# Patch embedding of a vision transformer: small inputs in whole rows, the weights' column sums as two rows in front of the images

## The chip, the cores and the metric

One core of a Trainium2 chip runs one program. The metric is the device time of one execution in microseconds (us). TensorE is written PE, VectorE DVE, ScalarE ACT, GpSimd POOL, SyncE SP. SP and ACT also issue the DMA transfers.

## The reference, cut to what matters

```python
# x: (16, 3, 96, 96) images, patches of 16x16 pixels, 6x6 per image
patches = x.reshape(B, C, h, P, w, P).transpose(0, 2, 4, 3, 5, 1).reshape(B, h * w, P * P * C)
y = _layernorm(patches, ln1_w, ln1_b)                 # over 768 numbers of a patch
y = jnp.einsum('bnp,pd->bnd', y, lin_w) + lin_b       # (768, 256)
y = _layernorm(y, ln2_w, ln2_b)
y = jnp.concatenate([cls, y], axis=1)                 # 37 tokens an image, 592 in all
y = y + pos_embedding[:, :n + 1]
...
h = _L0_tok_ref(...)
h = h + _L0_attn_ref(_layernorm(h), ...)              # 16 query heads, one key head
h = h + _L0_ffn_ref(_layernorm(h), ...)               # mixture of 8 experts, and a shared one
h = h + _L1_attn_ref(_layernorm(h), ...)              # three rounds over 16 heads, weights Wlq, Wlk, Wlv
h = h + _L1_ffn_ref(_layernorm(h), ...)               # quantised feed-forward
```

The change touches the first line of `h`, the patch stage, and the place at which products of the small matrices of `_L1_attn_ref` are made.

## The kernel before, in words

The program has one block for each engine, written out by hand in the order in which the engine runs it. There is no scheduler: engines meet at semaphores alone. PE writes into eight banks of PSUM, taken in a fixed order: `fills()` lists every fill of a bank with a key and the engine that empties it, fill n goes to bank n modulo 8, and `fill(key)` on PE first waits until fill n-8 is emptied. So the place of a key in the list sets who must have read what before PE may go on.

The first layer norm is folded into the embedding. The weights `lin_w` (six chunks `k` of 128 rows by 256) are scaled by `ln1_w` and a row of means is subtracted (`centred_weights`), and the patch's own rate 1/std is multiplied in behind the product (`rt`, `rtok`). The row of means and a constant row are column sums of `lin_w` weighted with `ln1_w` and `ln1_b`. The steps of the stage and their keys:

- `ln`: PE turns `ln1_w` and `ln1_b` into columns (`ln_cols`), ACT copies them.
- `ad`: a product of a 0/1 matrix (`token_of`) with `table` (position, class token and `ln2_b`, one row per token of an image) gives for each of five tiles of 128 tokens what is added to it (`addend`). DVE builds `table` in `make_table` once `pos_in` says that ACT's three small transfers have landed.
- `xp`: the patches of channel c are copied together by POOL (four of six columns of patches) and ACT (`windows`, two of six), turned by PE (four fills of three transposes each) and copied by ACT into `patT`.
- `cs`: the column sums. `mr`, `cr`: they are turned and spread over 128 partitions; ACT makes `mean_row` of the first, DVE `c_row` of the second.
- `y`: the embedding, tiles 0 and 1 chunk by chunk, then 2 and 3, then 4. `rt` stands between.
- `wl`, `wn`, `bl`: block-diagonal copies of Wlq, Wlk, Wlv, which DVE puts into `wlT`; `pw`: two rounds of products of them (their powers); `wc`: the key and query weights of the fourth stage multiplied with them; `xT`: the turned normalised tokens.

All loads of weights stand on SP's queue, ahead of the images or behind them, in the order of the code; nothing of the stage but the five small transfers is on ACT's queue.

Of the kernel before, what the change touches and what calls it, by code (L numbers as in the profile page):

```python
# [84 lines left out]
POOL_WINDOWS = 4  # L85

# [3 lines left out]
def fills():  # L90
# [21 lines left out]
    f.extend((("pw", n), "act") for n in range(2))  # L112
# [15 lines left out]
    f.extend((("wc", n), "act") for n in ("q", 1, 2, 3))  # L128
# [76 lines left out]
def build(nc, i, out):  # L205

    with ExitStack() as ctx:
# [3 lines left out]
        def sem(name):  # L211
            return ctx.enter_context(nc.semaphore(name))
# [13 lines left out]
        def cut(region, n):  # L226
            at[0] += n
            return region[:, at[0] - n:at[0]]
# [68 lines left out]
        col_sums = cut(cur, 4)  # L297
# [18 lines left out]
        r_lin, r_ln2w, r_ln2b = (sqr_all[:, n * D:(n + 1) * D] for n in range(3))  # L316
        rsd_all = sb("rsd", P, NR * CF)
        rsd = rsd_all[:, :].rearrange("p (n t) -> p n t", n=NR)
        token_all = rsd_all[0:T, 0:NP]
        token_of = rsd_all[0:T, 0:NT].rearrange("p (b t) -> p b t", t=T)  # L320
# [4 lines left out]
        table = probs_all[0:T, 0:DA]  # L325
        r_cls = probs_all[0:T, 2 * D:3 * D]
# [80 lines left out]
        weights_centred = sem("weights_centred")  # L407
        attn_cleared = sem("attn_cleared")
# [65 lines left out]
        def _(sp):  # L474
# [57 lines left out]
        def _(pool):  # L532
            links = [0]

            def link(ins):
                links[0] += 1
                ins.then_inc(pool_chain, 1)
                pool.wait_ge(pool_chain, links[0])
# [29 lines left out]
            link(pool.memset(token_all[:, NT:NP], 0.0))  # L568
            pool.tensor_copy(token_of, ident[0:T, 0:T].unsqueeze(1).to_broadcast([T, B, T])).then_inc(consts_ready, 1)  # L569
# [78 lines left out]
        def _(act):  # L648
# [44 lines left out]
            b = take(act, ("ln",))  # L693
            empty(act.copy(ln_cols.rearrange("p c v k -> p (c v k)"), b[:, 0:4 * NC]))
# [3 lines left out]
            windows(0)  # L698
            channel(0)
            b = take(act, ("cs",))  # L700
            empty(act.copy(col_sums, b[:, 0:4]))
            b = take(act, ("mr",))
            empty(act.mul(mean_row, b[:, 0:D], 1.0 / PV))
            for c in (1, 2):
                windows(c)
                channel(c)
# [39 lines left out]
            for n in range(2):  # L746
                powers(n)
# [57 lines left out]
            for n in ("q", 1, 2):  # L805
                composed_weights(n)
# [174 lines left out]
        def _(dve):  # L981
# [33 lines left out]
            def make_table():  # L1015

                dve.wait_ge(pos_in, 48)
                dve.tensor_reduce(table[:, D + 1:DA], ident[0:T, 1:T].rearrange("p (g w) -> p w g", g=NG), AX.X, ALU.add)  # L1018
                dve.tensor_scalar(first[:, 1:2], ident[0:T, 0:1], -1.0, 1.0, ALU.mult, ALU.add)
                link(dve.tensor_copy(first[:, 0:1], ident[0:T, 0:1]))  # L1020
                link(dve.scalar_tensor_tensor(out=table[:, 0:D], in0=r_cls, scalar=first[:, 0:1], in1=table[:, 0:D],
                                              op0=ALU.mult, op1=ALU.add))
                dve.tensor_copy(table[:, D:D + 1], first[:, 1:2])
                link(dve.scalar_tensor_tensor(out=table[:, 0:D], in0=r_ln2b[0:T, :], scalar=first[:, 1:2],
                                              in1=table[:, 0:D], op0=ALU.mult, op1=ALU.add))
                dve.tensor_copy(first[:, 0:1], ident[0:T, 0:1]).then_inc(table_ready, 1)  # L1026
# [58 lines left out]
            def rest_of_weights():  # L1085
                for k in range(4, PK):
                    centred_weights(k)
# [10 lines left out]
            variance_given(ins, rest_of_weights)  # L1098
# [579 lines left out]
        def _(pe):  # L1678
# [10 lines left out]

            def full(ins):  # L1690
                ins.then_inc(bank_filled, 1)
# [14 lines left out]

            b = fill(("ln",))
            keep_awake(b, 6)
# [5 lines left out]

            pe.wait_ge(table_ready, 1)
            for t in range(TT):
                b = fill(("ad", t))
                full(product(b[:, 0:DA], [(token_all[:, t * P:(t + 1) * P], table)]))
# [14 lines left out]
            channel(0)  # L1733
# [3 lines left out]
            for n in range(2):  # L1737
                ins = product(b[:, 2 * n:2 * n + 2], [(lin_w[:, k, n * P:(n + 1) * P], ln_cols[:, k // 2, :, k % 2]) for k in range(PK)])
            full(ins)
            emptied(pe, ("cs",))  # L1740
            for v, key in enumerate((("mr",), ("cr",))):
                b = fill(key)
                for n in range(2):
                    ins = pe.transpose(b[:, n * P:(n + 1) * P], col_sums[:, 2 * n + v:2 * n + v + 1].to_broadcast([P, P]), ident[:, :])
                full(ins)
            channel(1)
            channel(2)

# [20 lines left out]
            bs_ = [fill(("y", t)) for t in range(2)]  # L1769
            for k in range(PK):  # L1770
                pe.wait_ge(weights_centred, k + 1)
                for g in range(2):
                    emptied(pe, ("xp", k, g))
                for t in range(2):
                    ins = pe.matmul(bs_[t][:, 0:D], patT[:, k, t * P:(t + 1) * P], lin_w[:, k, :], start=(k == 0), stop=(k == PK - 1))  # L1775
                    if k == PK - 1:
                        full(ins)

# [8 lines left out]
            pe.wait_ge(image_of_ready, 1)  # L1787
# [25 lines left out]
            emptied(pe, ("bl",))  # L1813
            for n in range(2):
                if n:
                    emptied(pe, ("pw", 0))
# [158 lines left out]

            composed_weights("q", "q1", q_)
            for n in range(2):
                emptied(pe, ("pw", n))
            for a in (1, 2, 3):
                composed_weights(a, "k1", KEY_POWER[a - 1])  # L1980
# [258 lines left out]
```

## Time and profile before

| what | us |
|---|---|
| median of 3 runs | 324.23 (324.05 to 325.01) |
| the profiled execution, its time | 322.2 |
| the same, its span in the trace | 320.5 |
| PE busy in the span | 264.7 |
| DVE busy | 201.6 |
| ACT busy | 100.4 |
| POOL busy | 45.0 |

The span runs from the first to the last instruction of the program. The time has 1.7 us more around it. All times in the rows below are counted from the span's start. The granted clock of TensorE in the rows is a share of 2.4 GHz: 1.00 is the upper level, 0.50 is 1.2 GHz.

### The profile page before, as it was taken

How to read it: one execution, taken by the hardware profiler on the slowest of the kernel's cores; microseconds unless marked ns; L12 is line 12 of the kernel's file. 1: busy time of each engine (PE TensorE's matmuls, PEld its weight loads, DVE VectorE, ACT ScalarE, POOL GpSimd, SP SyncE). 2: the span in 40 equal slices, each digit the busy share in tenths (PEclk: the TensorE clock that was granted, in tenths of full speed). 3: DMA queues.
4: the chain of work that ended last, by engine and by line, in shares of the span. 5: the costliest groups of instructions: out<-in, count | busy, mean ns of one | idle time of the engine just before them, and what ended most of it. 6: DMA issues, size and time to landing. Idle time of an engine off the chain costs nothing.

```text
span 320.5 us, 5617 instructions
## 1 busy us (share of the span) xinstructions
PE 264.7 (83%) x2221; PEld 218.8 (68%) x2221; DVE 201.6 (63%) x485; ACT 100.4 (31%) x238; POOL 45.0 (14%) x88
## 2 busy tenths in 40 slices
PE   4039699678987989999999998998868899937496
PEld 3028688578977757777787798876646677717484
DVE  1051608953683536889788962786788846997931
ACT  1004610333224154211111253476330533917000
POOL 7140000020053000000000000679400000000000
PEclk9999979879557999999999986999999999987789
DMA  7919500500000043000000000000000000000011
GB/s 205 221 22 314 169 2 1 164 3 2 4 0 2 4 149 146 2 0 0 0 2 1 0 2 1 2 3 0 4 0 3 0 0 2 0 0 0 1 35 43
DMA packets 14524, 12.10 MB, mean 38 GB/s; under 512 B 2975, under 2 KB 13954, under 8 KB 14498
## 3 DMA queue, kind: packets, MB, share of 16 engines
q1 hardware_dynamic: 14376, 11.62, 12.3%
q8 instruction: 18, 0.29, 0.4%
q10 hardware_dynamic: 122, 0.12, 0.1%
q14 instruction: 8, 0.07, 0.1%
HBM read 11.13 MB, written 0.61 MB: 37 GB/s over the span
## 4 chain that ended last, share of the span: by engine, by line
PE 66%; DVE 18%; ACT 6%; DMA 5%; issue 3%; ACTq 1%; DVEq 0%
PE bank L1702 47%; DMA sqr<-in_L_tok_ln_b 5%; PE bank L2206 5%; PE bank L1865 3%; PE bank L1898 2%; DVE part L1546 2%; PE bank L1775 2%; PE bank L1929 2%; DVE big L1610 1%; DVE keys_n L1591 1%; PE bank L1840 1%; PE bank L1973 1%; DVE big L1644 1%; ACT xT L740 1%; PE bank L1729 1%
## 5 line engine op out<-in xcount | busy, mean ns | idle before, releaser
L1702 PE MATMUL bank<-xT,big 128*128 128x296 f32 (+1 forms) x192 | 45.7, 391 | 0.0
L1702 PEld LDWEIGHTS bank<-xT,big 128*128 128x128 f32 x192 | 34.3, 190 | 9.5 <-issue 0.2
L1702 PE MATMUL bank<-xT,fT 128*128 128x296 f32 (+12 forms) x96 | 24.6, 416 | 0.6 <-DVE xT L1567 0.6
L1702 PE MATMUL bank<-big,cur 128*128 128x256 f32 (+1 forms) x100 | 23.3, 381 | 0.7 <-DVE cur L1321 0.7
L822 ACT ACTIVATE cen<-bank 128x296 f32<-128x296 f32 x20 | 8.3, 418 | 46.4 <-PE bank L1702 40.7
L1697 PE MATMUL bank<-ident,ones 128*128 128x128 f32 x100 | 17.1, 340 | 6.2 <-POOL rsd L569 4.4
L1702 PEld LDWEIGHTS bank<-xT,fT 128*128 128x128 f32 x96 | 17.2, 191 | 7.1 <-issue 2.1
L1702 PEld LDWEIGHTS bank<-big,cur 128*128 128x128 f32 (+1 forms) x100 | 18.0, 182 | 4.9 <-DVE cur L1321 1.5
L1697 PEld LDWEIGHTS bank<-ident,ones 128*128 128x128 f32 x100 | 16.4, 253 | 6.6 <-POOL rsd L569 4.4
L1334 DVE SCALAR_TENSOR_TENSOR h<-bank,route,h 128x256 f32<-128x256 f32 (+1 forms) x40 | 17.0, 478 | 2.8 <-PE bank L1702 2.8
L624 POOL TENSOR_SCALAR big<-keys_n,k_w 128x256 f32<-128x256 f32 x24 | 17.5, 750 | 6.4 <-DVE keys_n L1425 6.4
L1546 DVE TENSOR_REDUCE part<-big 128x1 f32<-128x296 f32 (+2 forms) x18 | 13.1, 731 | 6.3 <-ACT big L958 6.3
L1702 PE MATMUL bank<-probs,rsd 37*128 37x263 f32 x10 | 4.7, 658 | 13.4 <-DVE first L1026 13.4
L2206 PE MATMUL bank<-fT,big 128*128 128x256 f32 (+1 forms) x60 | 15.2, 419 | 0.6 <-DVE big L1543 0.6
L2206 PEld LDWEIGHTS bank<-fT,big 128*128 128x128 f32 (+1 forms) x60 | 12.2, 206 | 3.4 <-DVE big L1543 0.8
L1702 PEld LDWEIGHTS bank<-probs,rsd 37*128 37x128 f32 x10 | 3.2, 327 | 14.4 <-DVE first L1026 13.5
L616 POOL COPY cur<-xT 128x256 f32<-128x256 f32 x2 | 0.8, 404 | 80.9 <-ACT xT L742 80.9
L1321 DVE TENSOR_TENSOR cur<-cen,bank 128x296 f32<-128x296 f32 x20 | 9.1, 461 | 4.8 <-PE bank L1702 4.4
L1702 PE MATMUL bank<-wT_o,att 128*128 128x256 f32 (+1 forms) x40 | 9.3, 383 | 1.5 <-DVE att L1502 0.9
L606 POOL TENSOR_TENSOR big<-big,row_sum 128x370 f32<-128x370 f32 x8 | 6.2, 813 | 24.8 <-DVE row_sum L1217 24.8
L1702 PEld LDWEIGHTS bank<-wT_o,att 128*128 128x128 f32 (+1 forms) x40 | 7.0, 182 | 3.1 <-DVE att L1502 1.3
L1018 DVE TENSOR_REDUCE probs<-ident 37x6 f32<-37x36 f32 x1 | 0.2, 208 | 14.2 <-DMA sqr<-in_L_tok_ln_b 14.2
(312 smaller groups left out, 540.2 us busy)
## 6 DMA issues: line engine op xcount, KB each, us to landing
big<-in_x SPq DMA_DIRECT2D x3, 576.0 KB, 11.8
big<-in_L_ffn_w_gate SPq DMA_DIRECT2D x2, 512.0 KB, 6.5
big<-in_L_ffn_w_up SPq DMA_DIRECT2D x2, 512.0 KB, 6.7
big<-in_L_ffn_w_down SPq DMA_DIRECT2D x1, 1024.0 KB, 5.5
small<-in_L_tok_lin_w SPq DMA_DIRECT2D x3, 256.0 KB, 5.5
small<-in_L_ffn_w_gate SPq DMA_DIRECT2D x1, 768.0 KB, 4.6
small<-in_L_ffn_w_up SPq DMA_DIRECT2D x1, 768.0 KB, 6.8
small<-in_L_ffn_w_down SPq DMA_DIRECT2D x1, 768.0 KB, 8.1
```

Of the source, the lines that this page charges most:

```text
L624: ins = pool.tensor_scalar(fkeys[a - 1][:, u, :, n, :], keys, k_w[:, a - 1, n:n + 1], 1.0, ALU.mult, ALU.mult)
L822: empty(act.activation(silu[:, c, :], b[:, 0:HP], ACT.Silu))
L1321: empty(dve.tensor_tensor(hid[:, e % 3, c * HP:(c + 1) * HP], silu[:, c, :], b[:, 0:HP], ALU.mult))
L1334: ins = dve.scalar_tensor_tensor(out=v, in0=src, scalar=route[0:n, t, e:e + 1], in1=v, op0=ALU.mult, op1=ALU.add)
L1546: return dve.tensor_reduce(part[:, n:n + 1], v, AX.X, ALU.max, apply_absolute_value=True)
L1697: pe.matmul(b[:, 0:P], ones[:, :], ident[:, :], start=True, stop=True)
L1702: ins = pe.matmul(out_, a_, b_, start=(n == 0), stop=(n == len(pairs) - 1))
L1775: ins = pe.matmul(bs_[t][:, 0:D], patT[:, k, t * P:(t + 1) * P], lin_w[:, k, :], start=(k == 0), stop=(k == PK - 1))
L1865: ins = pe.matmul(b[32 * j:32 * j + m, at_:at_ + 4 * T].rearrange("p (u c) -> p u c", u=2), w(k), xq[:, k, :, 2 * j * T:2 * (j + 1) * T], ...
L1898: ins = pe.matmul(bs_[j][:, (2 * t + s) * T:(2 * t + s + 1) * T], qT[rows, row:row + P], kT[rows, u, s * T:(s + 1) * T], start=True, stop= ...
L1929: ins = pe.matmul(b[32 * q:32 * q + 32, m * 2 * T:(m + 1) * 2 * T].rearrange("p (i t) -> p i t", i=2), vals[0:G3, 3 * u + g, s, h_, :], by ...
L2206: ins = pe.matmul(b[0:rows, 0:D], gate[:, o * NT + t * P:o * NT + t * P + rows], fT[2][:, o, :], start=(o == 0), stop=(o == FC - 1))
```

## The change

Four things are changed.

1. ACT's small transfers: position rows 0 to 31 and 32 to 36 as two transfers, the class token and `ln2_b` as one row each (rows 37 and 38 of `table`, which gets `TR` = 39 rows), and these ahead of `ln1_w` and `ln1_b`. `token_of` gets two more rows (from `row_of`, two short POOL instructions), so that the product `ad` adds class token and `ln2_b`; `make_table` keeps two instructions and waits for no transfer. PE waits for `pos_in` itself.
2. The column sums are two rows of 256 (`ln_cols` is the stationary operand, `lin_w` moves) in place of four columns of 128, and are spread with a product in place of two transposes.
3. `lin_w` is loaded ahead of the images, and `ad`, `ln`, `cs`, `mr`, `cr` stand ahead of all of `xp`. DVE centres chunks 0 to 3 (with the statistics of channel 1 between), POOL chunks 4 and 5. The embedding of tiles 0 and 1 begins with chunks 0 and 1 ahead of channel 2.
4. The two fills `pw` move from behind `wkvT` to between the fills `wc`.

```diff
-    f = [(("ln",), "act")]
-    f.extend((("ad", t), "act") for t in range(TT))
-    channel(0)
+    f = [(("ad", t), "act") for t in range(TT)]
+    f.append((("ln",), "act"))
     f.append((("cs",), "act"))
     f.append((("mr",), "act"))
     f.append((("cr",), "dve"))
+    channel(0)
     channel(1)
     channel(2)
...
-    f.extend((("pw", n), "act") for n in range(2))
...
-    f.extend((("wc", n), "act") for n in ("q", 1, 2, 3))
+    f.extend((key, "act") for key in (("pw", 0), ("wc", "q"), ("pw", 1), ("wc", 1), ("wc", 2), ("wc", 3)))
...
+            for n in range(NC):
+                sp.dma_start(lin_w[:, 2 * n:2 * n + 2, :], lw[n]).then_inc(patch_w_in, 16)
             for c in range(NC):
                 sp.dma_start(imv[0:96, c, :], im[c]).then_inc(images_in[c], 16)
-                if c == 0:
-                    for n in range(NC):
-                        sp.dma_start(lin_w[:, 2 * n:2 * n + 2, :], lw[n]).then_inc(patch_w_in, 16)
...
+            emptied(pool, ("ln",))
+            emptied(pool, ("mr",))
             pool.wait_ge(windows_pool, NC * POOL_WINDOWS)
+            for k in range(DVE_CHUNKS, PK):
+                v = lin_w[:, k, :]
+                link(pool.tensor_scalar(v, v, ln_cols[:, k // 2, 0, k % 2:k % 2 + 1], 1.0, ALU.mult, ALU.mult))
+                pool.tensor_tensor(v, v, mean_row, ALU.subtract).then_inc(weights_centred_pool, 1)
...
+            for lo, hi in ((0, 32), (32, T)):
+                act.dma_start(table[lo:hi, 0:D], i["L0_tok_pos_embedding"][0, lo:hi, :]).then_inc(pos_in, 16)
+            act.dma_start(table[T:T + 1, 0:D], i["L0_tok_cls_token"][0, 0:1, :]).then_inc(pos_in, 16)
+            act.dma_start(table[T + 1:TR, 0:D], i["L0_tok_ln2_b"].unsqueeze(0)).then_inc(pos_in, 16)
             for n, name in enumerate(("L0_tok_ln1_w", "L0_tok_ln1_b")):
                 act.dma_start(ln_rows[2 * n:2 * n + 2, :], i[name].rearrange("(k m) -> k m", k=2)).then_inc(ln_in, 16)
-            act.dma_start(table[:, 0:D], i["L0_tok_pos_embedding"][0, :, :]).then_inc(pos_in, 16)
-            act.dma_start(r_cls, i["L0_tok_cls_token"][0, 0, :].partition_broadcast(T)).then_inc(pos_in, 16)
-            act.dma_start(r_ln2b[0:T, :], i["L0_tok_ln2_b"].partition_broadcast(T)).then_inc(pos_in, 16)
...
-            channel_statistics(1)
             emptied(dve, ("mr",))
             emptied(dve, ("ln",))
-            for k in range(4):
+            for k in range(DVE_CHUNKS):
+                if k == 2:
+                    channel_statistics(1)
                 centred_weights(k)
             link(channel_statistics(2))
...
-            for n in range(2):
-                ins = product(b[:, 2 * n:2 * n + 2], [(lin_w[:, k, n * P:(n + 1) * P], ln_cols[:, k // 2, :, k % 2]) for k in range(PK)])
-            full(ins)
+            full(product(b[0:2, 0:D], [(ln_cols[:, k // 2, :, k % 2], lin_w[:, k, :]) for k in range(PK)]))
             emptied(pe, ("cs",))
             for v, key in enumerate((("mr",), ("cr",))):
                 b = fill(key)
-                for n in range(2):
-                    ins = pe.transpose(b[:, n * P:(n + 1) * P], col_sums[:, 2 * n + v:2 * n + v + 1].to_broadcast([P, P]), ident[:, :])
-                full(ins)
+                full(product(b[:, 0:D], [(ident[0:2, v:v + 1].to_broadcast([2, P]), col_sums)]))
+            channel(0)
             channel(1)
+            first_banks = [opened(("y", t)) for t in range(2)]
...
+            embedding_of_first(range(2))
             channel(2)
+            for t in range(2):
+                fill(("y", t))
+            embedding_of_first(range(2, PK))
```

PE before, from the column sums (`lin_w` is in tensor `small`, `patT` in `big`, the patches of channels 0 to 2 in `fT0` to `fT2`) to the first products of the embedding:

```order
L1702 MATMUL bank2<-cur,small 128x2 [waits patch_w_in,act_emptied]
L1702 MATMUL bank2<-cur,small 128x2 x11
L1744 MATMUL bank3<-ident,cur 128x128 [waits act_emptied]
...
L1729 MATMUL bank0<-ident,fT1 128x96 [waits act_emptied]
...
L1729 MATMUL bank3<-ident,fT2 128x96 [waits act_emptied,windows_act,windows_pool]
L1729 MATMUL bank3<-ident,fT2 128x96 x2
L1729 MATMUL bank4<-ident,fT2 128x96 [waits dve_emptied]
L1729 MATMUL bank4<-ident,fT2 128x96 x2
L1775 MATMUL bank5<-small,big 128x256 [waits act_emptied,weights_centred]
```

And PE in the change, from `ad` to the same place:

```order
L1707 MATMUL bank0<-probs,rsd 128x263 [waits pos_in,table_ready]
...
L1707 MATMUL bank6<-small,cur 2x256 [waits patch_w_in,act_emptied]
L1707 MATMUL bank6<-small,cur 2x256 x5
L1707 MATMUL bank7<-cur,ident 128x256 [waits act_emptied]
L1707 MATMUL bank0<-cur,ident 128x256 [waits act_emptied]
...
L1735 MATMUL bank7<-ident,fT1 128x96 [waits act_emptied,windows_act,windows_pool]
L1735 MATMUL bank7<-ident,fT1 128x96 x2
L1735 MATMUL bank0<-ident,fT1 128x96 [waits dve_emptied]
L1735 MATMUL bank0<-ident,fT1 128x96 x2
L1761 MATMUL bank5<-small,big 128x256 [waits weights_centred,act_emptied,image_of_ready]
L1761 MATMUL bank6<-small,big 128x256
```

The fill that waits for DVE to empty `cr` was the last of channel 2, `fT2` into bank 4; now it is the last of channel 1, `fT1` into bank 0, with two chunks of the embedding and all of channel 2 behind it.

DVE in the change, from the statistics of channel 0 to `c_row`, which empties `cr`:

```order
L1069 BN_STATS st<-big 96x6 [waits images_in0]
L1069 BN_STATS st<-big 96x6 x5
L1073 SCALAR_TENSOR_TENSOR small<-small,cur 128x256 [waits act_emptied]
L1073 SCALAR_TENSOR_TENSOR small<-small,cur 128x256
L1069 BN_STATS st<-big 96x6 [waits images_in1]
L1069 BN_STATS st<-big 96x6 x5
L1073 SCALAR_TENSOR_TENSOR small<-small,cur 128x256 x2
L1069 BN_STATS st<-big 96x6 [waits images_in2]
L1069 BN_STATS st<-big 96x6 x5
L1085 BN_AGGR mv<-st 96x2 [waits dve_chain]
L1085 BN_AGGR mv<-st 96x2 x5
L1090 TENSOR_TENSOR cur<-bank0,sqr 128x256 [waits bank_filled,norm_rows_in]
```

Before, the statistics of channels 0 and 1 stood ahead of the wait for `mr`, four chunks followed it, then channel 2, the six aggregates, two more chunks and `c_row`.

## Rows read from the trace of the kernel before

**Rows 1.** Chain of work that ended last: start us, us, what.

```profile
2.47 17.11 DMA sqr<-in_L_tok_ln_b
...
21.25 4.75 PE bank L1702 x10
...
28.21 4.98 PE bank L1702 x24
...
34.58 1.67 DVE small L1072 x4
36.25 1.98 DVE st L1068 x6
...
38.40 0.55 DVE mv L1083 x5
...
39.68 0.35 DVE cur L1090
...
47.43 8.90 PE bank L1702 x46
```

**Rows 2.** DMA queues from 8 to 12 us: packets, MB, share of 16 engines.

```profile
q10 hardware_dynamic: 29, 0.03, 3.2%
```

**Rows 3.** The page's DMA issues: KB each, median us to landing.

```profile
big<-in_x SPq DMA_DIRECT2D x3, 576.0 KB, 11.8
small<-in_L_tok_lin_w SPq DMA_DIRECT2D x3, 256.0 KB, 5.5
```

**Rows 4.** Timeline to 66 us: start, us, engine, line, operation, [idle before <-releaser].

```profile
3.52 0.13 POOL L568 MEMSET rsd<- 37x48 f32 x1
4.44 2.93 PE L1697 MATMUL bank<-ident,ones 128*128 128x128 f32 x12 [4.44 <-POOL rsd L569]
7.30 0.50 PE L1712 MATMUL bank<-ident,cur 4*128 4x4 f32 x3
22.56 0.47 SPq L503 DMA_DIRECT2D gate_w<-in_L_ffn_gate_w  x1
34.34 2.97 PE L1729 MATMUL bank<-ident,fT 96*128 96x96 f32 x18
40.07 0.47 PE L1729 MATMUL bank<-ident,fT 96*128 96x96 f32 x3 [1.75 <-DVE cur L1090]
40.37 7.06 PE L1775 MATMUL bank<-small,big 128*128 128x256 f32 x24
```

**Rows 5.** PE's line of the first embedding, two stretches: PE busy, records, granted clock.

```profile
40.50:43.70 3.20, 3.20 (x8) 0.50 0.02 5
44.00:47.20 3.20, 3.20 (x16) 1.00 0.00 0
```

**Rows 6.** Timeline, 62 to 70 us.

```profile
62.59 1.69 DVE L1043 TENSOR_SCALAR xn<-h,mv,rstd 128x256 f32<-128x256 f32 x5
62.73 1.65 PE L1702 MATMUL bank<-wlT 128*128 128x128 f32 x6 [2.82 <-DVE bl L1117]
67.25 1.52 PE L1840 MATMUL bank<-ident,xn 128*128 128x128 f32 x10
68.20 1.54 ACT L740 COPY xT<-bank 128x256 f32<-128x256 f32 x6 [1.08 <-PE bank L1840]
```

**Rows 7.** The chain again, the query projections.

```profile
69.84 8.88 PE bank L1865 x271
```

**Rows 8.** PE's line L1929 alone (32 columns a piece), two stretches, as in rows 5.

```profile
98.50:101.80 3.30, 3.30 (x121) 0.50 0.02 5
105.80:107.90 2.10, 2.10 (x128) 1.00 0.03 8
```

**Rows 9.** Timeline, the fills `wc` of the second place.

```profile
111.16 3.73 PE L1702 MATMUL bank<-wlT,small 128*128 128x128 f32 x32
114.53 0.29 ACT L672 ACTIVATE var<-mv,eps_c 128x5 f32<-128x5 f32 x1
```

**Rows 10.** Timeline, POOL and DVE together in the fourth stage.

```profile
202.69 2.88 POOL L624 TENSOR_SCALAR big<-keys_n,k_w 128x256 f32<-128x256 f32 x3
202.78 1.99 DVE L1393 TENSOR_TENSOR big<-keys_n,k_w 128x1536 f32<-128x1536 f32 x1
```

More of the change, by code:

```diff
@@ L85 @@
 POOL_WINDOWS = 4
+DVE_CHUNKS = 4
+TR = T + 2
 def fills():
@@ L315, in build @@
         sqr = sqr_all[:, :].rearrange("p (n t) -> p n t", n=NR)
-        r_lin, r_ln2w, r_ln2b = (sqr_all[:, n * D:(n + 1) * D] for n in range(3))
+        r_lin, r_ln2w = (sqr_all[:, n * D:(n + 1) * D] for n in range(2))
         rsd_all = sb("rsd", P, NR * CF)
         rsd = rsd_all[:, :].rearrange("p (n t) -> p n t", n=NR)
-        token_all = rsd_all[0:T, 0:NP]
-        token_of = rsd_all[0:T, 0:NT].rearrange("p (b t) -> p b t", t=T)
+        token_all = rsd_all[0:TR, 0:NP]
+        token_of = rsd_all[0:TR, 0:NT].rearrange("p (b t) -> p b t", t=T)
         cmpa, cmpb = (rsd_all[:, n * TT * NE * NE:(n + 1) * TT * NE * NE].rearrange(
@@ L324, in build @@
         probsT = [x[0:G3, 0:3 * R].rearrange("p (g r) -> p g r", g=3) for x in (cur, probs_all)]
-        table = probs_all[0:T, 0:DA]
-        r_cls = probs_all[0:T, 2 * D:3 * D]
+        table = probs_all[0:TR, 0:DA]
+        row_of = probs_all[0:TR, 2 * D:2 * D + T]
         fprobs, fheads = (probs_all[:, n * 2 * CF:(n + 1) * 2 * CF].rearrange(
@@ L407, in build @@
         weights_centred = sem("weights_centred")
+        weights_centred_pool = sem("weights_centred_pool")
         attn_cleared = sem("attn_cleared")
@@ L567, in _ @@
             pool.memset(h[64:P, TT - 1, :], 0.0)
-            link(pool.memset(token_all[:, NT:NP], 0.0))
-            pool.tensor_copy(token_of, ident[0:T, 0:T].unsqueeze(1).to_broadcast([T, B, T])).then_inc(consts_ready, 1)
+            pool.memset(token_all[:, NT:NP], 0.0)
+            pool.tensor_tensor(row_of[:, 0:1], ident[0:TR, 0:1], ident[0:TR, T:T + 1], ALU.add)
+            link(pool.tensor_tensor(row_of[:, 1:T], ident[0:TR, 1:T], ident[0:TR, T + 1:TR].to_broadcast([TR, T - 1]), ALU.add))
+            pool.tensor_copy(token_of, row_of.unsqueeze(1).to_broadcast([TR, B, T])).then_inc(consts_ready, 1)
             pool.memset(patT_bt[:, :, :, 0], 0.0)
@@ L691, in channel @@
                         empty(act.copy(patch_columns(k, g), patches_turned(b)))
-            b = take(act, ("ln",))
-            empty(act.copy(ln_cols.rearrange("p c v k -> p (c v k)"), b[:, 0:4 * NC]))
             for t in range(TT):
@@ L697, in _ @@
                 empty(act.copy(addend[:, t, :], b[:, 0:DA]))
-            windows(0)
-            channel(0)
+            b = take(act, ("ln",))
+            empty(act.copy(ln_cols.rearrange("p c v k -> p (c v k)"), b[:, 0:4 * NC]))
             b = take(act, ("cs",))
-            empty(act.copy(col_sums, b[:, 0:4]))
+            empty(act.copy(col_sums, b[0:2, 0:D]))
             b = take(act, ("mr",))
             empty(act.mul(mean_row, b[:, 0:D], 1.0 / PV))
-            for c in (1, 2):
+            for c in range(NC):
                 windows(c)
@@ L803, in weight_turned @@
                     empty(act.copy(fT[2][:, 2 * j:2 * j + 2, :], b[:, :].rearrange("p (c o) -> p c o", c=2)))
-            for n in ("q", 1, 2):
-                composed_weights(n)
+            powers(0)
+            composed_weights("q")
+            powers(1)
+            composed_weights(1)
+            composed_weights(2)
             inverse_root(P, slice(0, TT))
@@ L1015, in make_table @@
             def make_table():
[L1017 to L1026, printed above, removed]
+                dve.tensor_reduce(table[:, D + 1:DA], ident[0:TR, 1:T].rearrange("p (g w) -> p w g", g=NG), AX.X, ALU.add)
+                dve.tensor_copy(table[:, D:D + 1], ident[0:TR, T + 1:TR]).then_inc(table_ready, 1)
             def statistics(ts):
@@ L1083, in _, with constant_row @@
                 ins = dve.bn_aggr(mv[0:96, w, :], st[0:96, 3 * w:3 * w + 3, :].rearrange("p a b -> p (a b)"))
-            def rest_of_weights():
-                for k in range(4, PK):
-                    centred_weights(k)
+            def constant_row():
                 dve.wait_ge(norm_rows_in, 32)
@@ L1688, in fill, with opened @@
                 return banks[n % 8]
+            def opened(key):
+                emptied(pe, FILLS[FILL[key] - 8][0])
+                return bank_of(key)
             def full(ins):
@@ L1705, in _ @@
             pe.wait_ge(consts_ready, N_CONSTS)
+            for t in range(TT):
+                b = fill(("ad", t))
+                if t == 0:
+                    keep_awake(b, 4)
+                    pe.wait_ge(table_ready, 1)
+                    pe.wait_ge(pos_in, 64)
+                full(product(b[:, 0:DA], [(token_all[:, t * P:(t + 1) * P], table)]))
             b = fill(("ln",))
-            keep_awake(b, 6)
             pe.wait_ge(ln_in, 32)
@@ L1713, in _ @@
             full(ins)
[L1715 to L1718, printed above, removed]
             def channel(c):
@@ L1731, in channel @@
                         full(ins)
-            channel(0)
             b = fill(("cs",))
@@ L1742, in _, with embedding_of_first @@
                 b = fill(key)
-                for n in range(2):
-                    ins = pe.transpose(b[:, n * P:(n + 1) * P], col_sums[:, 2 * n + v:2 * n + v + 1].to_broadcast([P, P]), ident[:, :])
-                full(ins)
+                full(product(b[:, 0:D], [(ident[0:2, v:v + 1].to_broadcast([2, P]), col_sums)]))
+            channel(0)
             channel(1)
+            first_banks = [opened(("y", t)) for t in range(2)]
+            def embedding_of_first(ks):
+                for k in ks:
+                    if k < DVE_CHUNKS:
+                        pe.wait_ge(weights_centred, k + 1)
+                    else:
+                        pe.wait_ge(weights_centred_pool, k + 1 - DVE_CHUNKS)
+                    for g in range(2):
+                        emptied(pe, ("xp", k, g))
+                    for t in range(2):
+                        ins = pe.matmul(first_banks[t][:, 0:D], patT[:, k, t * P:(t + 1) * P], lin_w[:, k, :],
+                                        start=(k == 0), stop=(k == PK - 1))
+                        if k == PK - 1:
+                            full(ins)
+            pe.wait_ge(image_of_ready, 1)
+            embedding_of_first(range(2))
             channel(2)
+            for t in range(2):
+                fill(("y", t))
+            embedding_of_first(range(2, PK))
             def small_matrices():
@@ L1767, in small_matrices @@
                 full(product(b[:, 0:2 * NH], [(bq8.rearrange("p n d -> p (n d)"), ident[0:2 * NH, 0:2 * NH])]))
[L1769 to L1777, printed above, removed]
             def embedding(ts):
@@ L1785, in embedding @@
                 full(ins)
-            pe.wait_ge(image_of_ready, 1)
             b = fill(("rt",))
@@ L1812, in _, with powers @@
             q_, k_, v_, nk, nv = range(5)
[L1813 to L1816, printed above, removed]
+            def powers(n):
                 b = fill(("pw", n))
@@ L1974, in weight_turned @@
                 full(ins)
+            emptied(pe, ("bl",))
+            powers(0)
             composed_weights("q", "q1", q_)
[L1977 to L1980, printed above, removed]
+            emptied(pe, ("pw", 0))
+            powers(1)
+            composed_weights(1, "k1", KEY_POWER[0])
+            composed_weights(2, "k1", KEY_POWER[1])
+            emptied(pe, ("pw", 1))
+            composed_weights(3, "k1", KEY_POWER[2])
             turn(1, 2)
```

5 lines of the change are left out of this document (2 added, 3 removed).

## Prediction

> **What bounds the kernel now.** I read the chain of waits first, since the change is at the program's start. Its first piece says it all: ACT's last small transfer (`ln2_b`, 37 rows) is issued at 2.47 us and landed 17.11 us later, at 19.6 [rows 1]. PE waits for the table made of it; the product `ad` starts at 21.25 and from there the chain runs on PE with short pieces of ACT and DVE. Next I asked why 111 rows of 1 KB take so long. ACT's queue (q10) moves 29 packets in the four microseconds from 8 to 12 [rows 2], one in 0.14 us: a row at a time, one behind the other. The weights `lin_w` (three transfers of 256 KB) need 5.5 us each in the same crowd, the images 11.8 us in the median [rows 3].
>
> The Trainium skill says why (DMA: Bandwidth & Descriptors, section "Why a DMA increments its semaphore by 16 and not by 1"): a transfer runs on the largest number of engines up to 16 that divides its slowest dimension, so 37 rows run on one and 32 on 16. The trace agrees for 37, by the drip just shown; for 32 nothing here shows it.
>
> Third, the timeline of PE up to 66 us [rows 4]. To about 37 us PE is slow: 18 transposes of 96 columns take 2.97 us, 0.16 each, while three at 40.07 take 0.47 in all, tails included. The clock rows say 1.00 there, but the durations say 1.2 GHz. At 40.07 PE resumes after 1.75 us in which a bank waited for DVE to read `cr`; behind it 24 records of the embedding run at 0.40 us apiece under a granted clock of 0.50 and at 0.20 under 1.00 [rows 5]. The embedding ends near 56.3 us (47.43 and 8.90, rows 1).
>
> **The change, step by step, on the clock of the profiled execution.**
>
> *Start of `ad`.* POOL has two more short instructions and a link ahead of `token_of`: a short one beside it takes 0.13 us [rows 4], so I take 0.35 us, and PE starts at 4.8 in place of 4.44. Four warming products are 8 records of the 12 that took 2.93 us: 1.95 us, so 6.75. `ad` can start then, if the table has landed. Now 32 rows, then 5, then 1 and 1 are ahead of all else on ACT. At one packet in 0.14 us even all 39 rows in one file last 5.5 us from an issue at 0.8: 6.3, plus a start of some 1 us that I read off the first landings (PE had `ln` at 7.30 at the latest). I take 6.75, bound by PE; the high bound is 9. `ad` takes 4.75 us as before [rows 1] and ends at 11.5. Before, this was 26.0.
>
> *To `mean_row`.* `ln` 0.50 [rows 4], ACT's copy 0.2: 12.2. `cs`: 12 records with 256 moving columns, as many as the embedding's. At 0.43 (low clock) 5.1, plus 0.2: 17.5. At the upper clock it would be 2.6. I take the low one, since what PE does ahead of it is what it did before at low speed. It replaces 4.98 us [rows 1], so the two-row form by itself is worth nothing. ACT's copy 0.4, one spread (2 records, tail) 1.05, ACT 0.4: `mean_row` stands at 19.45, in place of 34.58. **Minus 15.1 us** so far. `lin_w`, now first on SP, has landed some 5.5 us after its issue, 6 us early; the images, issued by 5 us and landing by about 16 as before, are early too.
>
> *The new stall.* This is the step that the short description does not tell. `xp` of channel 1 now ends in the bank of `cr`, which DVE empties last. From `mean_row` DVE has four chunks (1.67), statistics of channel 1 and of channel 2 (1.98 each, the second with a link of 0.15), aggregates 0.55 and `c_row` 0.35, with gaps 6.8 us [rows 1]. Before, it was 5.5, to 40.07. PE meanwhile has only the spread of `cr` and 21 transposes of 0.16, so it idles about 3 us. And POOL works on chunks 4 and 5 at the same time. Where POOL and DVE both read two things from SBUF, at 202.7, POOL's three take 2.88 us, 0.96 each, and DVE's 1.99 [rows 10]; so one of the two was held up. I add 0.5 us; the bounds are 0 and 1.9 (two of POOL's instructions). Resumption at 26.75 in place of 40.07: **minus 13.3**.
>
> The skill has a rule against this (SBUF — State Buffer, the rules on the shared port pair): a DVE instruction with two SBUF inputs and a GpSimd one that reads SBUF exclude one another for the whole instruction. By it the centring, not the statistics, could be held; the rows at 202.7 agree that something is, and my bounds already have room for it.
>
> *From there to the end of the first embedding.* Before, 3 transposes and 24 records took 40.07 to 47.27: 7.2 us, with the first 3.4 at low clock. Now 15 transposes and the same 24 records: at the upper clock 15 times 0.083 and 24 times 0.216, 6.45 us (0.083 is 0.16 halved with the clock, 0.216 is 5.2 over 24). PE comes from an idle stretch, as before, so the clock is low at first. The earlier case cost 1.7 us for it; I take 2.2, and 0.2 for latencies: 8.85. Ends at 35.6 in place of 47.27: **minus 11.7**. ACT has the last channel copied in that time: four copies and a `windows` are 2.7 us and PE gives it 6. `rt`, tiles 2 to 4 and everything on DVE behind them follow as before (8.90 us of PE, rows 1): the last of the attention's weights was issued at 22.56 [rows 4], by the 5.5 us above it had landed near 28, and is wanted after 44.
>
> *`pw` moved.* Its first fill held PE from 62.73 and the second ended near 66.6; then warming, and transposes at 67.25, though the first `xn` was there at about 63.0 [rows 6]. Now the transposes pace with `xn` (1.69 us for five): PE begins at 63.05, at low clock 10 records of 0.21 end at 65.3, ACT's copies (1.54 for all) at 65.9, and the projections can start at 66.1, not 69.84: minus 3.75. But what warmed the clock was `pw`. The projections, 8.88 us [rows 7], now start at low clock. Pieces of 32 columns run at 3.30 over 121 and 2.10 over 128, 27.3 and 16.4 ns, at the two levels [rows 8], so a low stretch loses 40% of its length. After the resumption at 40.07 the clock was low for 3.5 us or a little more; here I choose 4.7 us as the middle of 2.5 and 7, somewhat less and twice as much, for PE comes from sparse work. That costs 1.0 to 2.8; I take 1.9. At the new place the two fills, 12 records, stand ahead of the third `wc`, whose copy ACT must make ahead of the root that DVE waits for. There 32 records take 3.73, 0.117 each [rows 9]: plus 1.4. Together **minus 0.45**.
>
> **Sum:** minus 11.7 minus 0.45, 12.1 us. The profiled execution would be 322.2 minus 12.1, 310.1. It was 2.0 us under the median 324.23, so the median follows at **312.1**.
>
> **Rivals.**
>
> *Clock and port kinder.* Low clock nowhere longer than before, no hold by POOL, and `cs` partly at the upper level (PE then has 128 full rows moving, unlike before). Minus 2.2, 0.5, 1.9 and 1.0 at most; half to all of it gives 306.5 to 309.3. For it speaks that pieces at low clock were always followed by a rise when PE ran full (rows 5 and 8).
>
> *Low clock longer.* The projections all at low clock, or the embedding up to `rt`: 8.88 times 0.66 is 5.9, less the 1.9 counted, plus 4.0; the embedding the same, 12.6 less 8.85, plus 3.8. One gives 316. Against it: rows 8 rise with just such pieces.
>
> *Small transfers still late.* They now run beside 768 KB of `lin_w`. Each microsecond of landing behind 6.75 is one of the end. Landed at 10: 315.4. Landed at 19, as now, gives 324.4: the change would then not do what it says. Against it: 39 rows in place of 111.
>
> *Slower than before.* One mechanism: PE never leaves the low clock from the resumption to the end of the projections. The first embedding costs 3.8 more, `rt` and 36 records 8.9 more, the projections 4.0: 16.7, so 328.8. It decides once the low clock has cost 12.1 us more than counted, some 24 us of PE's work at half speed in a row. The rise by 44.0 in the same products [rows 5] speaks against it.
>
> **How the numbers follow.** The forecast has 0.55, with its own range of 309.5 to 314.5; kinder 0.17, longer low clock 0.17, late transfers 0.08 (of it 0.02 for no change), slower 0.03. The range 308.0 to 316.5 leaves out the best part of the kinder case and the worst of the late and slow ones, together under 0.2. Within 0.3% is within 1 us, about what a measurement of this kernel can tell. Faster 0.95, same 0.02, slower 0.03.
>
> **What would show it.** In the profile after: `ad` begins at 6.5 to 7.5 with no wait for a transfer; `cs` of 12 records lasts about 5 us; `mean_row` at 19 to 20; PE's wait for DVE's `c_row` of about 3 us, ending at 26 to 28, in the middle of channel 1; `rt` near 36; the projections start near 54, and their length is over 10 us. Wrong it would be by a wait of PE for `pos_in` behind 9 us, by a bank that I have not seen, or by a clock that stays at 0.50 in the embedding.

## The result, and the profile after

The changed kernel takes 309.58 us in the median of 4 runs (305.52 to 309.95), the kernel before 324.14 beside it (4 runs, 323.09 to 325.01): ratio 0.9524, 95% interval 0.9439 to 0.9608. Forecast were 312.1 and a range of 308.0 to 316.5. The profiled execution took 309.35 with a span of 307.6, 12.9 us under the span of 320.5 before; the sum had said 12.1. Run again (c0) it gave 308.40 against 322.69, ratio 0.9551 (0.9510 to 0.9593). Medians are of all executions, but ratios leave out those over 1.5% above the fastest of their kernel: two of e3's six (306.75 and 308.77), one of e7's six (304.88, the profiled one) and one of e5's four (508.8, the profiled one).

The chain of waits of the changed kernel, start, us and what, from the landing that opens it to the first projections; it answers to [rows 1]:

```profile
2.14 4.88 DMA probs<-in_L_tok_ln_b
...
7.16 4.72 PE bank L1707 x10
...
12.57 5.29 PE bank L1707 x12
...
19.45 1.10 DVE small L1073 x2
20.55 1.96 DVE st L1069 x6
22.51 0.78 DVE small L1073 x2
23.30 1.98 DVE st L1069 x6
...
26.34 0.74 PE bank L1735 x3
27.08 3.47 PE bank L1761 x8
30.55 1.58 PE bank L1735 x12
32.12 3.48 PE bank L1761 x16
35.61 8.90 PE bank L1707 x46
...
54.04 9.50 PE bank L1876 x272
...
93.38 6.86 PE bank L1707 x48
```

Read it against the old chain. The first piece was 17.11 us long and is 4.88. `ad` starts at 7.16 in place of 21.25. Then comes a stretch of DVE from 19.45 to 26.34, 6.9 us; in the old chain the same wait for `c_row` was 5.5 us long (34.58 to 40.07). PE has 21 transposes to do in it and is idle for the rest. The embedding of tiles 0 and 1 ends near 35.6, in place of 47.4 (`rt`, whose first product overlaps its end, starts at 35.44, in place of 47.27). The projections start at 54.04, not 69.84.

PE's timeline in the same kernel shows the wait itself, answering to [rows 4]:

```profile
19.36 1.84 PE L1735 MATMUL bank<-ident,fT 96*128 96x96 f32 x18
22.68 0.71 PE L1735 MATMUL bank<-ident,fT 96*128 96x96 f32 x3 [1.48 <-issue]
26.34 0.74 PE L1735 MATMUL bank<-ident,fT 96*128 96x96 f32 x3 [2.95 <-DVE cur L1090]
```

The last three transposes of channel 1 stand behind 2.95 us of idle time, ended by DVE's `c_row` (L1090). The 1.48 us ahead of 22.68 end with ACT's part of the channel's patches (its copy runs from 21.94 to 22.59); the profile names no releaser for them. The busy times by stretch give the clock (PE, PEld, DVE, ACT and POOL busy with their records, then the granted clock):

```profile
18.00:21.30 3.30, 2.90 (x22) 2.23 (x22) 1.85 (x5) 2.52 (x6) 1.62 (x3) 1.00 0.08 2
21.50:26.20 4.70, 0.71 (x3) 0.45 (x3) 4.67 (x19) 2.71 (x6) 2.88 (x5) 0.50 0.98 320
26.40:31.50 5.10, 5.10 (x19) 4.28 (x20) 0.00 (x0) 1.54 (x3) 0.00 (x0) 0.50 0.95 276
31.70:35.40 3.70, 3.70 (x21) 3.31 (x20) 0.00 (x0) 1.91 (x6) 0.00 (x0) 1.00 0.76 248
```

The clock was at the upper level behind the 12 wide records of `cs`: the 18 transposes at 19.36 take 0.10 us each, and at the low level they took 0.16. PE was then busy for 0.71 us of 4.70, the clock fell, and 5.1 us of full work ran at the low level before it rose.

### The profile page after: what moved, and what is told of

The parts are those of the page before. It is cut to its first block, busy times and chain, and to the rows that moved or that the text cites. A ratio compares the mean times of both kernels' runs of the same rounds, so it can differ in the third digit from the quotient of the medians.

```text
span 307.6 us, 5589 instructions
## 1 busy us (share of the span) xinstructions
PE 262.7 (85%) x2205; PEld 211.9 (69%) x2205; DVE 199.6 (65%) x478; ACT 100.4 (33%) x238; POOL 48.1 (16%) x94
## 4 chain that ended last, share of the span: by engine, by line
PE 68%; DVE 19%; ACT 6%; issue 3%; DMA 2%; ACTq 1%; DVEq 0%
PE bank L1707 49%; PE bank L2221 5%; PE bank L1876 3%; PE bank L1909 3%; DVE part L1546 2%; PE bank L1761 2%; PE bank L1940 2%; DMA probs<-in_L_tok_ln_b 2%; DVE big L1610 1%; DVE st L1069 1%; DVE keys_n L1591 1%; PE bank L1984 1%; DVE big L1644 1%; ACT big L980 1%; DVE xn L1044 1%
## 5 line engine op out<-in xcount | busy, mean ns | idle before, releaser
L1702 PE MATMUL bank<-ident,ones 128*128 128x128 f32 x96 | 15.7, 329 | 6.7 <-POOL rsd L572 4.8
L1702 PEld LDWEIGHTS bank<-ident,ones 128*128 128x128 f32 x96 | 14.7, 240 | 7.1 <-POOL rsd L572 4.8
L1851 PE MATMUL bank<-ident,xn 128*128 128x128 f32 x40 | 7.1, 305 | 4.1 <-DVE xn L1044 3.9
L1044 DVE TENSOR_SCALAR xn<-h,mv,rstd 128x256 f32<-128x256 f32 x20 | 7.0, 406 | 4.0 <-ACT rstd L683 4.0
L1909 PE MATMUL bank<-kT,qT 16*128 16x37 f32 x160 | 8.0, 374 | 1.1 <-ACT qT L763 1.1
```

Source lines behind the costliest of these rows:

```text
L1044: dve.tensor_scalar(xn[:, t, :], h[:, t, :], mv[:, t, 0:1], rstd[:, t:t + 1], ALU.subtract, ALU.mult).then_inc(xn_ready, 1)
L1702: pe.matmul(b[:, 0:P], ones[:, :], ident[:, :], start=True, stop=True)
L1851: ins = pe.transpose(b[:, at_:at_ + P], xn[:, t, k * P:(k + 1) * P], ident[:, :])
L1909: ins = pe.matmul(bs_[j][:, (2 * t + s) * T:(2 * t + s + 1) * T], qT[rows, row:row + P], kT[rows, u, s * T:(s + 1) * T], start=True, stop= ...
```

## The experiments

Each kernel was run beside the kernel before on its chip: c0 and e1 to e3 on one, e4 to e7 on another, e8 and e9 on a third. Kernels are compared by their ratio to it. Where a diff is cut, `...` marks it.

**The changed kernel again (c0), as yardstick.**

> The changed kernel once more, as the yardstick for its neighbours on the same chip. Both theories: 309.6, within the spread of the first runs (305.5 to 310.0).

308.40 (305.93 to 309.99), as expected.

**The transfers alone (e1).** The kernel before with part 1 and nothing else (of its diff, the transfers):

```diff
...
-            act.dma_start(table[:, 0:D], i["L0_tok_pos_embedding"][0, :, :]).then_inc(pos_in, 16)
-            act.dma_start(r_cls, i["L0_tok_cls_token"][0, 0, :].partition_broadcast(T)).then_inc(pos_in, 16)
-            act.dma_start(r_ln2b[0:T, :], i["L0_tok_ln2_b"].partition_broadcast(T)).then_inc(pos_in, 16)
+            for lo, hi in ((0, 32), (32, T)):
+                act.dma_start(table[lo:hi, 0:D], i["L0_tok_pos_embedding"][0, lo:hi, :]).then_inc(pos_in, 16)
+            act.dma_start(table[T:T + 1, 0:D], i["L0_tok_cls_token"][0, 0:1, :]).then_inc(pos_in, 16)
+            act.dma_start(table[T + 1:TR, 0:D], i["L0_tok_ln2_b"].unsqueeze(0)).then_inc(pos_in, 16)
...
```

> The kernel before with part 1 alone (small transfers in 32, 5, 1 and 1 rows, a table of 39 rows). Theory 'the transfer is all': PE warms with 12 records from 4.8 to 7.7, ln 0.5, ad starts at about 8.25 in place of 21.25, everything behind moves by 13.0 us: 324.1 - 13.0 = 311.1, and parts 2 and 3 together are worth nothing, since the resumption after the wait for c_row then comes at about 27.1. Rival 'the reordering carries part of it': with the images not ahead of the column sums the stage must be shorter; then this kernel is slower than the changed one by clearly more than the 1.7 us of the moved powers, 313 or more. A second rival: the later images become the bound once the table is early; then PE waits for POOL's patches behind ad.

308.51, ratio 0.9572 (0.9544 to 0.9601): the whole gain, within what can be told from the changed kernel's 0.9551. Both rivals fall. PE's timeline:

```profile
8.07 4.75 PE L1698 MATMUL bank<-probs,rsd 39*128 39x263 f32 x10
26.90 0.54 PE L1726 MATMUL bank<-ident,fT 96*128 96x96 f32 x3 [1.76 <-DVE cur L1086]
34.10 1.18 PE L1698 MATMUL bank<-rstd,cen 96*128 96x6 f32 x10
```

`ad` starts 0.9 us later than in the changed kernel and PE resumes 0.6 later, yet `rt` comes at 34.10, against 35.44 there. The old order leaves 3 transposes and 24 records behind the wait, the new one 15 and 24, with more of it at the low clock. So with this wait in place parts 2 and 3, the reordering of the stage, gained nothing, and in these profiles lost 1.3 us by this point.

What e1 doesn't separate: part 1 moves 39 rows in place of 111, replaces the two broadcasts by one row each, and takes DVE's work on the table (19.60 to 21.21, 1.6 us of the chain before) out of the way. `ad` starts 13.2 us earlier by all three; the broadcasts alone were not tried.

**`pw` back at its old place (e2).**

```diff
+    f.extend((("pw", n), "act") for n in range(2))
...
-    f.extend((key, "act") for key in (("pw", 0), ("wc", "q"), ("pw", 1), ("wc", 1), ("wc", 2), ("wc", 3)))
+    f.extend((("wc", n), "act") for n in ("q", 1, 2, 3))
...
```

> The changed kernel with the two fills pw back at their old place. The prediction's term (minus 0.45 for the move): 0.5 us slower than the changed kernel, about 310.1. The trace of the changed kernel (projections start 3.6 us earlier in relation to the end of the embedding, lose 0.6 to the clock, and the second place costs 1.34) says 1.7 us slower: 311.3. Rival: the clock decides and the move is worth nothing or less, 309.6 or under.

309.69, ratio 0.9621 (0.9586 to 0.9656), against 0.9551 for c0: 2.3 us worse by the ratios, 1.3 by the medians, and the intervals just touch. The chain of e2:

```profile
35.37 8.90 PE bank L1707 x46
...
58.22 9.06 PE bank L1881 x272
...
68.54 2.44 PE bank L1914 x80
...
95.77 5.52 PE bank L1707 x36
...
105.05 2.33 PE bank L1707 x8
```

and of c0:

```profile
35.40 8.90 PE bank L1707 x46
...
53.79 9.59 PE bank L1876 x272
...
64.50 3.46 PE bank L1909 x80
...
94.89 6.86 PE bank L1707 x48
...
105.51 2.33 PE bank L1707 x8
```

The move brings the projections forward by 4.4 us. Of this 0.5 is lost in the projections, 1.0 in the first scores and 1.4 in the 24 products behind them (4.18 us against 2.80), which run at a lower clock, and 1.34 at the new place; at the gate's products (105) this profile of the changed kernel is 0.46 us behind. So in one pair of profiles the move is worth nothing, in the medians one to two microseconds. Its sign is not settled; the forecast of minus 0.45 lies between.

e2 is also the kernel before with parts 1, 2 and 3, so beside e1 it weighs parts 2 and 3 alone. Its first embedding ends at 35.37 against 34.26, its projections start at 58.22 against 57.10, and its median is 309.69 against 308.51: 1.1 to 1.2 us slower each time.

**`c_row` ahead of the statistics of channel 1 (e3).**

```diff
                 if k == 2:
+                    dve.wait_ge(norm_rows_in, 32)
+                    b = take(dve, ("cr",))
+                    empty(dve.tensor_tensor(c_row, b[:, 0:D], r_lin, ALU.add))
                     channel_statistics(1)
...
-            def constant_row():
-                dve.wait_ge(norm_rows_in, 32)
-                b = take(dve, ("cr",))
-                empty(dve.tensor_tensor(c_row, b[:, 0:D], r_lin, ALU.add))
...
-            variance_given(ins, constant_row)
+            variance_given(ins)
```

> The changed kernel with DVE's c_row ahead of the statistics of channel 1, so that the bank of cr is empty at about 20.9 us. Theory 'a new stall': PE's idle 2.95 us in the middle of channel 1 goes, and the end of the first embedding comes 2 to 3 us earlier: 307. Rival 'it only moves': ACT's copies or the clock take what the stall gives up, 309 to 309.6.

304.02, ratio 0.9392 (0.9360 to 0.9425), better than c0 by 5.1 us by the ratios and by 4.4 us by the medians of all six executions of each; expected were 2 to 3. The stall was real. PE's timeline of e3:

```profile
21.98 1.19 PE L1733 MATMUL bank<-ident,fT 96*128 96x96 f32 x6 [1.18 <-issue]
23.11 3.75 PE L1759 MATMUL bank<-small,big 128*128 128x256 f32 x8
31.24 1.18 PE L1705 MATMUL bank<-rstd,cen 96*128 96x6 f32 x10
```

The wait for DVE is gone and `rt` starts at 31.24, 4.0 us before c0's 35.24. That is more than the idle time of 2.95. Some 0.6 us come from the clock behind the stretch (12 transposes in 1.27 us, against 1.91 in c0), and 0.4 from ahead of it: in e3 the 12 records of `cs` took 4.91 us in place of 5.28, and in e9 below 4.46, as the clock rose before they ended. What is left of idle time, the 1.18 us ahead of 21.98, ends with ACT's copy of patches (21.24 to 21.88).

**All six chunks on DVE (e4).**

```diff
-DVE_CHUNKS = 4
+DVE_CHUNKS = 6
```

> The changed kernel with all six chunks centred on DVE, none on POOL. If POOL's share is worth what it takes from DVE (two chunks, 0.84), c_row and with it PE's resumption come 0.84 later, less the 0.25 by which DVE's first two chunks ran longer beside POOL (1.10 in place of 0.85): 0.6 us slower than the changed kernel, in the trace a resumption at 26.6 to 26.9. Rival 'the shared port costs more than it gives': resumption not later than 26.3.

306.30, ratio 0.9542 (0.9486 to 0.9598), no different from c0. In the trace PE resumes at 26.56, against 26.00 in c0: the expected 0.6. DVE's first two chunks take 0.88 us alone and 1.10 beside POOL:

```profile
19.10 0.88 DVE L1073 SCALAR_TENSOR_TENSOR small<-small,cur 128x256 f32<-128x256 f32 x2 [6.98 <-ACT cur L711]
```

and in c0:

```profile
19.11 1.10 DVE L1073 SCALAR_TENSOR_TENSOR small<-small,cur 128x256 f32<-128x256 f32 x2 [8.30 <-ACT cur L711]
```

So beside POOL DVE loses 0.2 us, not the 0.5 that I had added; in the changed kernel's first profile one of the four instructions lasted 0.70 us and the others 0.46 to 0.48. The Trainium skill (SBUF — State Buffer, section "SBUF: two separate sides") says that of a DVE instruction with two SBUF inputs and a GpSimd one that reads SBUF the second waits until the first has finished. The sign fits; how the 0.2 us comes about no run here shows.

**One transfer of 37 rows (e5).**

```diff
-            for lo, hi in ((0, 32), (32, T)):
-                act.dma_start(table[lo:hi, 0:D], i["L0_tok_pos_embedding"][0, lo:hi, :]).then_inc(pos_in, 16)
+            act.dma_start(table[0:T, 0:D], i["L0_tok_pos_embedding"][0, :, :]).then_inc(pos_in, 16)
...
-                    pe.wait_ge(pos_in, 64)
+                    pe.wait_ge(pos_in, 48)
```

> The changed kernel with the position rows as one transfer of 37 rows. Theory 'number of rows in one file': 39 rows in one file at 0.09 to 0.14 us from about 2 us land at 6.5 to 8 us, ad starts 0 to 1 us later than the changed kernel's 6.8 to 7.2, 308.4 to 309.4. Rival 'the split in 32 and 5 is what matters': ad later than 9 us, and the end later by as much.

305.39, ratio 0.9467 (0.9437 to 0.9498). The profiled execution of e5 is the one of 508.8 us, in which PE ran at half speed or less from the first embedding on (the other three took 305.2 to 305.6). Its first 7 us are like the others: the warming takes 2.02 us (2.08 in c0), and `ad` starts at 6.83, straight behind it. So 37 rows as one transfer are in time, and the split in 32 and 5 buys no time. It does bring the rows earlier: up to 4 us ACT's queue had moved 58 of its 70 packets in c0, and 25 of 50 in e5. But PE is busy with its warming until 6.8. What mattered is that fewer rows stand in this queue, 39 in place of 111. That the ratio is 2.7 us better than c0's I can't explain: it rests on three executions, all of the lower kind (below), and no row of its trace speaks for it.

**Sums as columns (e6).**

```diff
...
-            full(product(b[0:2, 0:D], [(ln_cols[:, k // 2, :, k % 2], lin_w[:, k, :]) for k in range(PK)]))
+            for n in range(2):
+                ins = product(b[:, 2 * n:2 * n + 2], [(lin_w[:, k, n * P:(n + 1) * P], ln_cols[:, k // 2, :, k % 2]) for k in range(PK)])
+            full(ins)
...
```

> The changed kernel with the column sums in the form of before (24 short records with two columns). The prediction said the form is worth nothing by itself: cs 4.98 in place of 5.1 to 5.3, so mean_row 0.3 earlier. But in the traces the clock rose at 18 us at the end of the new form and not behind the old one. Theory 'form worth nothing': 308.1 to 308.7, end of the first embedding as in the changed kernel within 0.5 us. Rival 'it is what warms the clock': transposes of channel 0 at 0.16 instead of 0.08 to 0.10, but as PE then waits for c_row anyway, still nothing.

307.07, ratio 0.9540 (0.9504 to 0.9577): no difference from c0. The timeline tells what the form does to the clock:

```profile
12.23 5.28 PE L1707 MATMUL bank<-cur,small 128*128 128x2 f32 x24 [0.26 <-ACT cur L707]
18.67 3.09 PE L1735 MATMUL bank<-ident,fT 96*128 96x96 f32 x18
34.89 1.18 PE L1707 MATMUL bank<-rstd,cen 96*128 96x6 f32 x10
```

Both forms take 5.28 us. Behind the narrow one 18 transposes take 3.09 us, behind the wide one 1.84: only the wide one lifts the clock. It is so in every trace but e5's: with the wide form the 18 transposes take 1.84 us in five traces and 2.15 in e3, with the narrow one 2.90 to 3.09 in five. But PE waits for `c_row` next, and `rt` starts at 34.89 against 35.24.

**The order of before, with what pays (e7).** Part 1, part 4 and an early `c_row`, neither part 2 nor part 3:

```diff
...
             for k in range(4):
                 centred_weights(k)
+            dve.wait_ge(norm_rows_in, 32)
+            b = take(dve, ("cr",))
+            empty(dve.tensor_tensor(c_row, b[:, 0:D], r_lin, ALU.add))
             link(channel_statistics(2))
...
```

> The kernel before with part 1, part 4 and c_row ahead of the statistics of channel 2, and neither part 2 nor part 3: image 0 ahead of lin_w, channel 0 ahead of the column sums, no chunk on POOL. Theory 'parts 2 and 3 are worth nothing': as fast as the changed kernel with c_row early (304.0), since e1 had its embedding done 1.3 us earlier than the changed kernel and its stall of 1.76 us goes: 308.5 - 1.3 - 1.8 to 3.4, 303.8 to 305.4. Rival 'they pay once the stall is gone': 306 or more.

303.43 (300.17 to 304.88), ratio 0.9389 (0.9346 to 0.9433): the same as e3. The chains of e3 and of e7:

```profile
31.41 8.90 PE bank L1705 x46
...
50.12 9.10 PE bank L1874 x272
```

```profile
33.10 8.90 PE bank L1698 x46
...
51.25 9.97 PE bank L1860 x272
```

By the end of the first embedding e3 is 1.7 us ahead, at the start of the projections 1.1. So the medians are level, as 'worth nothing' had it, but the traces of this stage are not. Beside e1, e7 is 1.2 us ahead at that end (34.26) and 1.9 at the gate's products (103.50 and 101.59), so by this pair the move of `pw` is worth some 0.75 us there, where the other pair had minus 0.46; the medians differ by 5.1.

**More warming ahead of the projections (e8 on e7, e9 on e3).**

```diff
-            turn(0, 1, awake=2)
+            turn(0, 1, awake=7)
```

> e7 with seven warming products in place of two ahead of the transposes of the first normalised tokens (14 records, 3.0 us at the low clock, in a wait of PE that lasts about 2.5 us). Theory 'the lost pw warmed the clock': the granted clock is at the upper level when the projections start, they take 8.9 us, and the kernel gains 0.5 to 1 us on e7: 302.5 to 303.0. Rival 'the warming comes in the way of the transposes or changes nothing': 303.4 to 304.

> e3 (the changed kernel with c_row early) with the same seven warming products. By the first theory 303.0 to 303.5, by the rival 304.0 or more. Beside e8 it says again whether parts 2 and 3 are worth anything once the stall is gone: by 'nothing' the two are within 1 us.

e8: 305.11, ratio 0.9439 (0.9398 to 0.9479). e9: 301.95, ratio 0.9360 (0.9328 to 0.9393), the fastest of all. Both expectations missed, e8 to the slow side and e9 to the fast one. The chains of e8 and of e9:

```profile
33.07 8.90 PE bank L1698 x46
...
51.22 8.80 PE bank L1860 x272
```

```profile
30.73 11.22 PE bank L1705 x66
...
48.87 8.81 PE bank L1874 x272
```

The projections took 8.80 and 8.81 us, against 9.97 in e7 and 9.10 in e3, so the warming did what it was for; the first theory has that part. The end does not follow: e8 is not better than e7, e9 by its interval not clearly better than e3.

On parts 2 and 3 the pair says more. By 'nothing' e8 and e9 were to be within 1 us. e9 is 2.6 us ahead by the ratios, whose intervals do not meet, 2.3 us at the end of the first embedding and 2.3 at the start of the projections. With e3 and e7 that is two pairs of traces in which the reordering gains 1.7 and 2.3 us in the stage itself once `c_row` is early, after losing 1.1 with the wait in place (e2 and e1). At the end of the program one pair shows it and the other doesn't, so its worth there is not settled.

## Why the prediction was right, step by step

*Start of `ad`.* Forecast 6.75 with a bound of 9; 7.16 in the first profile, where the landing of the last small transfer decided, and 6.80 in c0, where PE's warming did. That part 1 alone brings this is shown by e1; its 1.6 us of DVE work included. The division of the rows that I had drawn on was not needed (e5).

*To `mean_row`.* Forecast 19.45, DVE starts at 19.45 (19.11 in c0). `cs` 5.28 against 5.3. That the numbers agree to the hundredth is luck: `ad` came 0.4 us late in this profile, the spread took 0.73 us in place of 1.05, and my terms add up to 19.35 and not to 19.45. That the two-row form is worth nothing by itself held in e6. I had left out that it warms the clock: in e3 and e9 this shortened `cs` itself by 0.4 and 0.8 us, and in the changed kernel it gained nothing, since PE had to wait behind it.

*The new stall.* Forecast: resumption at 26.75 after about 3 us idle, in the middle of channel 1. Measured 26.34 and 26.00, after 2.95. POOL's hold was sized at 0.5 and is 0.2. e3 shows the stall as cause: without it `rt` comes 4.0 us earlier and the projections 3.7 (50.12 against 53.79).

*To the end of the first embedding.* The forecast counts from the start of `rt`, 47.27 before, which is 35.44 after. Forecast 8.85 us, measured 9.10 (26.34 to 35.44). The low clock lasted 5.3 us behind the resumption and I had priced some 4.4. The resumption was 0.41 early and this stretch 0.25 long, so the errors cancel in part: 35.6 forecast, 35.44 measured.

*`pw`.* Start of the projections 15.45 us earlier forecast (11.7 and 3.75), 15.80 measured. The new place costs 1.34, forecast 1.4. The term that was mis-sized is the clock in the projections: 9.50 in place of 10.8 (8.88 plus 1.9), since it was low for 1.5 us or so of them (the mean granted clock from 54 to 64 us is 0.92) and not 4.7. Of my signs this one failed: I had named a length over 10 us, and it is 9.50, in c0 9.59.

*The rest.* By the first products behind the gate (107.36 against 121.13) the profile is 13.8 us ahead; at the end 12.9. The 0.9 lies in the later stages, where pieces fall differently on the stretches of low clock. The chain's piece of 132 records takes 14.56 in place of 13.48 at a mean granted clock of 0.79 in place of 0.86, the last products 15.77 in place of 15.18 at 0.84 in place of 0.87, and others are a little shorter. So the forecast of 12.1 is near the 12.9 in part because this loss, which I had not counted, takes back most of the 1.3 us that the projections gave.

The medians differ by 14.6 and the profiled spans by 12.9. The steps don't explain that. The profiled execution of the kernel before was 1.9 us under its median (322.2 and 324.14), and I carried this over to the changed kernel, whose profiled execution is 0.2 under (309.35 and 309.58). It is the spread of executions, and a part of it is visible. One kernel gives times of 306 to 307 and of about 310, in c0 three of each. In the stretch from 64 to 90 us, c0 (a run of 309.99) had this on PE:

```profile
64.00:90.00 26.00, 22.14 (x340) 0.54 0.01 2
```

and e4 (a run of 306.22), the same program there:

```profile
64.00:90.00 26.00, 21.50 (x445) 0.74 0.01 3
```

With a mean granted clock of 0.74 in place of 0.54 PE gets 445 records done and not 340. From the start of the projections to the gate's products this is 47.75 us against 51.72 (54.20 to 101.95, 53.79 to 105.51). It is not only these two: c0's three executions near 310 have a mean granted clock of 0.905 or 0.906 over the whole span, its three near 306 and 307 one of 0.911 to 0.915, and e3's six go the same way (302.1 to 304.5 at 0.915 to 0.920, 306.75 at 0.905, 308.77 at 0.900). In e7 and in the kernel before the times don't follow this mean. So differences of 1 or 2 us between kernels of this program are read from the traces at a landmark before 64 us, not from medians of six runs.

Of the rivals, the kinder clock had a share (projections), the longer low clock another (first embedding); late transfers, and the slower one, did not come.

## What to carry to other kernels

Look at what the chain's first piece is: here three small transfers, 111 rows one behind the other beside large loads, held the whole program to 19.6 us, and part 1 alone, which moves 39 rows, brought as much as all four parts together. When fills of a ring of banks are reordered, find for each the reader of the bank eight fills earlier and where it stands in its engine's order; the reordering of this stage turned an old wait of 1.75 us into one of 2.95 with more of PE's work at the low clock behind it, and one moved instruction brought `rt` 4 us forward. Only then did the reordering gain anything in its own stage. A gain on a PE that works in bursts comes partly as clock, so sum it at a landmark first and expect a microsecond or two either way behind it.

## What the runs showed of the hardware

- Twelve records with two stationary columns and 256 moving ones lifted the granted clock (18 transposes in 1.84 us behind them); 24 records with 128 stationary columns and two moving ones, 5.28 us without a pause as well, did not (3.09 us). In six traces and in five this was so each time.
- In these traces the page has a granted clock of 1.00 from the start, though PE runs at the low level until the first rise (0.16 us a transpose of 96 columns, 0.08 to 0.10 later).
- Executions of the changed kernel fall near 306 or near 310 (mean granted clock 0.915 to 0.911, or 0.906 to 0.905, in c0); in the two profiles compared, the difference goes with the share of low clock in the attention (0.74 or 0.54 from 64 to 90 us).
- Two fused DVE instructions with two SBUF operands took 1.10 us beside POOL's reads and 0.88 without (c0 and e4).
- With 37 rows of 1 KB as one transfer ACT's queue had moved 25 of its 50 packets by 4 us (e5), with the rows split in 32 and 5 it had moved 58 of 70 (c0).
